# Four strips at a time: scores and products of two units issued together in two attention stages

## The chip, the cores and the metric

The kernel runs on one core of one Trainium2 chip. What is measured is the device time of one execution of the whole program, in microseconds (us), of the slowest core; here that is the only one. A core has a matrix engine (TensorE, PE in the profile, with its weight loads as PEld), a vector engine (VectorE, DVE), a scalar engine (ScalarE, ACT), GpSimd (POOL) and queues for transfers (SyncE, SP). Each engine works through its own list of instructions in order, and they wait for one another by semaphores. TensorE writes to eight banks of PSUM, and the other engines read them from there.

## The reference, cut to what matters

A decoder of four layers with three sublayers each runs on x of 8 sequences x 256 tokens x 256 features, in float32. After each sublayer x becomes the normalised sum of x and the sublayer's result. Two of the twelve sublayers are touched, both in the last layer: a self-attention of 8 heads of 32, behind a normalisation of its own (the kernel calls it grouped), and a cross-attention of 16 heads of 16 over a context of 120 rows, with sigmoids in the place of the softmax.

```python
def _L3_attn_ref(x, Wq, bq, Wk, bk, Wv, bv, gamma, beta):      # H = 8, dk = 32
    ...
    q = (xn @ Wq + bq).reshape(B, S, H, dk).transpose(0, 2, 1, 3)
    k = (xn @ Wk + bk).reshape(B, S, H, dk).transpose(0, 2, 1, 3)
    v = (xn @ Wv + bv).reshape(B, S, H, D).transpose(0, 2, 1, 3)
    scores = jnp.einsum('bhsd,bhtd->bhst', q, k) / jnp.sqrt(jnp.asarray(dk, x.dtype))
    p = jax.nn.softmax(scores, axis=-1)
    att = jnp.einsum('bhst,bhtd->bhsd', p, v)
    out = att.reshape(S, B, D, H).sum(axis=-1).reshape(B, S, D)
    return out

def _L3_xattn_ref(q, k, v, Wq, Wk, Wv, gq, bq, gk, bk, Wp, bp):  # NUM_HEADS = 16, D = 16
    ...
    qh = _layernorm(qh, gq, bq) * scale
    kh = _layernorm(kh, gk, bk)
    attn = jax.nn.sigmoid(jnp.einsum('bhqd,bhkd->bhqk', qh, kh))
    x = jnp.einsum('bhqk,bhkd->bhqd', attn, vh)
    ...
    return x @ Wp.T + bp
```

## The kernel before

The program is one function per sublayer, one after the other. x stays on the chip. In both stages each engine has a loop over steps `t`, and in each step a fixed list of conditions says which piece of which batch or unit it issues; `at_step(t - a, every, count)` gives the piece's number when step `t` is its turn. So the order on every engine is written out by hand, and a piece that waits holds up everything behind it on its engine.

**Grouped attention** (`grouped_attention`, lines 3512 to 3855). A batch is one sequence of 256 tokens. A unit is two heads of one batch: 4 units to a batch, 32 in all, and two units are a quad (16 of them). The work of a unit, by function:

- `scores(u)` (line 3617), TensorE: four matmuls, two heads by two tiles of 128 query rows, each with 32 rows of contraction and 256 columns. The two heads lie on two different strips of 32 rows of the array. A float32 matmul shows as two passes, so a unit's scores are 8 MATMUL records. They go to two banks of PSUM, 0 and 1 for even units, 2 and 3 for odd ones. Unit `u` waits for the exponentials of unit `u - 2`.
- `maxima(u)` (3794), VectorE, then `exps(u)` (3715), ScalarE, from those banks into `probs`.
- `turn_probs(u)` (3629), TensorE: eight transposes into banks 4 and 5. It waits for the exponentials of its own unit and for both copies of the unit before.
- `store_probs(u)`: bank 4 is copied by ScalarE (3724), bank 5 by VectorE (3803). Each is the last piece of its step but for `store_k` on ScalarE.
- `products(u)` (3644), TensorE: four matmuls with 32 output columns each, on two strips of columns, 8 records, into bank 6. It waits for both copies of its unit, and in even units for `out_stored`.
- per quad: `store_out` (3730, ScalarE), `turn_out` (3651, TensorE), `normalise` (3811 and 3816, VectorE).

Once per batch come, through bank 7 and each waiting for the one before to have been copied out: `turn_x` (3578), `project("q")`, `project("k")`, `project_v` (these three through `mm`, line 461) and `turn_tail` (3603) on TensorE, with `store_x`, `store_k` and `store_tail` on ScalarE and `store_q` (3775) and `store_v` (3785) on VectorE. VectorE has besides `pre_statistics` (3751 to 3758), `pre_normalise`, `residual` (3824), `batch_statistics` (831 to 838) and `batch_normalise` (853) once per batch.

**Sigmoid attention** (`sigmoid_attention`, 3858 to 4165). A unit is four heads, 4 units to a batch, 32 in all. `scores(u)` (3962) is four matmuls on two strips of 32 rows, 8 records, again with banks 0 and 1 for even and 2 and 3 for odd units; `sigmoids(u)` (4045, ScalarE) reads them; `products(u)` (3977) is four matmuls, each on a column strip of its own. Per batch: `project_q`, `project_kv`, `output` (line 461), `turn_q` (3940), `turn_k` (3948) and `batch_turn` (862) on TensorE, `store_raw_q` (4015, 4018), `store_raw_k` and `store_q` (4035) on ScalarE, and `variance_q` to `residual` on VectorE.

Of the kernel before, what the change touches and what calls it, by code (L numbers as in the profile page):

```python
# [24 lines left out]
P = 128  # L25
B, L, D = 8, 256, 256
LC = 120
# [6 lines left out]
KT = D // P  # L34
# [839 lines left out]
def at_step(t, every, count):  # L874

    return t // every if t >= 0 and t % every == 0 and t // every < count else None
# [2635 lines left out]
def grouped_attention(nc, K):  # L3512
    W, S, A = weights_of(K, 9), K.S, Arena(K)
    H, HD = 8, 32
    PAIRS, LEAD = 4, 6
    UNITS, QUADS = B * PAIRS, B * PAIRS // 2
    BACK = LEAD + 12
    STEPS = PAIRS * (B - 1) + BACK + 3
    TB, X, Y = (4, 5), 6, 7

    qT, kT, xs = A(2, KT, L), A(2, KT, L), A(2, KT, L)
    vh, xn = A(2, 2, H, HD), A(2, 2, D)
    probs, probsT = A(2, 2, 2 * L), A(2, 2, 2 * L)
# [14 lines left out]
    def heads(u):  # L3538

        return [2 * (u % PAIRS) + s for s in range(2)]  # L3540

    with turn(nc, K) as block:
# [25 lines left out]
        def _(pe):  # L3568
# [35 lines left out]
                                                  K.x_tok[:, 2 * b + i, k * P:(k + 1) * P], K.ident[:])  # L3604
                ins.then_inc(S.aux_done, 1)

            def scores(u):
                b = u // PAIRS
                if u % PAIRS == 0:
                    pe.wait_ge(S.q_stored, b + 1)  # L3610
                    pe.wait_ge(S.k_stored, b + 1)
                if u >= 2:
                    pe.wait_ge(S.probs_done, u - 1)
                for i in range(2):
                    for s, h in enumerate(heads(u)):
                        rows = slice(HD * (h % 4), HD * (h % 4) + HD)
                        ins = nc.tensor.matmul(K.bank[2 * (u % 2) + s][:, i * L:(i + 1) * L],
                                               qT[rows, b % 2, h // 4, i * P:(i + 1) * P], kT[rows, b % 2, h // 4, :],
                                               start=True, stop=True)
                ins.then_inc(S.scores_done, 1)  # L3620

            def turn_probs(u):
                pe.wait_ge(S.probs_done, u + 1)
                for s in range(2):
                    if u:
                        pe.wait_ge((S.pair0_stored, S.pair1_stored)[s], u)
                    for k in range(2):
                        for i in range(2):
                            ins = nc.tensor.transpose(K.bank[TB[s]][:, k * L + i * P:k * L + (i + 1) * P],
                                                      probs[:, u % 2, s, i * L + k * P:i * L + (k + 1) * P], K.ident[:])  # L3630
                    ins.then_inc(S.probsT_done, 1)

            def products(u):
                b, n = u // PAIRS, u // 2
                pe.wait_ge(S.pair0_stored, u + 1)
                pe.wait_ge(S.pair1_stored, u + 1)
                if u % PAIRS == 0:
                    pe.wait_ge(S.v_stored, b + 1)
                if u % 2 == 0 and n:
                    pe.wait_ge(S.out_stored, n)  # L3640
                for k in range(2):
                    for s, h in enumerate(heads(u)):
                        rows = slice(HD * (h % 4), HD * (h % 4) + HD)
                        ins = nc.tensor.matmul(K.bank[X][rows, 0:L], vh[:, b % 2, k, h, :],
                                               probsT[:, u % 2, s, k * L:(k + 1) * L], start=k == 0, stop=k == 1)
                ins.then_inc(S.out_done, 1)

            def turn_out(n):
                pe.wait_ge(S.outT_stored, n + 1)
# [6 lines left out]
            for n, w in enumerate((W["gamma"], W["beta"])):  # L3656
                for k in range(KT):
                    ins = nc.tensor.transpose(K.bank[Y][:, 2 * n + k:2 * n + k + 1], w[0:1, 0, k * P:(k + 1) * P],
                                              K.ident[0:1, 0:1])
            ins.then_inc(S.aux_done, 1)  # L3660
            for t in range(STEPS):
                if (b := at_step(t - BACK - 2, PAIRS, B)) is not None:
                    turn_tail(b)
                if (u := at_step(t - LEAD, 1, UNITS)) is not None:
                    scores(u)
                if (b := at_step(t - 2, PAIRS, B)) is not None:
                    turn_x(b)
                if (b := at_step(t - 3, PAIRS, B)) is not None:
                    project("q", W["wq"], b)
                if (u := at_step(t - LEAD - 1, 1, UNITS)) is not None:  # L3670
                    turn_probs(u)
                if (n := at_step(t - LEAD - 4, 2, QUADS)) is not None:
                    turn_out(n)
                if (b := at_step(t - 4, PAIRS, B)) is not None:
                    project("k", W["wk"], b)
                if (b := at_step(t - 5, PAIRS, B)) is not None:
                    project_v(b)
                if (u := at_step(t - LEAD - 2, 1, UNITS)) is not None:
                    products(u)

        @block.scalar
        def _(a):
# [175 lines left out]
def sigmoid_attention(nc, K):  # L3858
    W, S, A = weights_of(K, 10), K.S, Arena(K)
    H, HD, PAD = 16, 16, 32  # L3860
    QUADS, LEAD = 4, 8
    UNITS = B * QUADS
# [24 lines left out]
    with turn(nc, K) as block:  # L3887
# [23 lines left out]
        def _(pe):  # L3911
# [37 lines left out]
                                              K.ident[0:LC, 0:LC])  # L3949
                ins.then_inc(S.aux_done, 1)  # L3950

            def scores(u):
                b, n = divmod(u, QUADS)
                if n == 0:
                    pe.wait_ge(S.q_stored, b + 1)
                    pe.wait_ge(S.k_stored, b + 1)
                if u >= 2:
                    pe.wait_ge(S.probs_done, u - 1)
                for s in range(2):
                    for r in range(2):  # L3960
                        rows = slice(PAD * (2 * (n % 2) + r), PAD * (2 * (n % 2) + r) + PAD)
                        ins = nc.tensor.matmul(K.bank[2 * (u % 2) + r][0:LC, s * L:(s + 1) * L],
                                               kz[rows, b % 2, s, n // 2, :], qT[rows, b % 2, n // 2, :],
                                               start=True, stop=True)
                ins.then_inc(S.scores_done, 1)

            def products(u):
                b, n = divmod(u, QUADS)
# [22 lines left out]
            for t in range(STEPS):  # L3991
                if (b := at_step(t - 7, QUADS, B)) is not None:
                    turn_k(b)
                if (b := at_step(t - BACK - 3, QUADS, B)) is not None:
                    batch_turn(nc, pe, K, b, Z)
                if (u := at_step(t - LEAD, 1, UNITS)) is not None:
                    scores(u)
                if (b := at_step(t, QUADS, B)) is not None:
                    project_q(b)
                if (b := at_step(t - 1, QUADS, B)) is not None:  # L4000
                    project_kv(b)
                if (b := at_step(t - 6, QUADS, B)) is not None:
                    turn_q(b)
                if (b := at_step(t - BACK, QUADS, B)) is not None:
                    output(b)
                if (u := at_step(t - LEAD - 1, 1, UNITS)) is not None:
                    products(u)
# [1089 lines left out]
```

## Time and profile before

| | us |
|---|---|
| median of 3 runs | 2608.3 (2607.41 to 2608.42) |
| the profiled execution | 2611.01 |
| its span in the trace | 2609.3 |
| PE busy | 2247.2 (86%) |
| DVE busy | 1418.8 (54%) |
| ACT busy | 1056.3 (40%) |
| mean clock granted to TensorE | 0.926 of full speed |

The span runs from the first to the last instruction of the trace. Grouped attention lies at about 1484 to 1672 us of it, sigmoid attention at about 1672 to 1837 us. Busy time is the union of an engine's instructions; an idle engine off the path that sets the time costs nothing. In a timeline a row is a run of like instructions on one engine: start, length from the first start to the last end, engine, line, operation, what it writes and reads, how many records, and in brackets how long the engine had been idle and what ended that. On TensorE a row's length includes the pipeline behind its last pass, so the next row may start before it ends.

### The profile page before, as it was taken

What the parts mean: (1) busy time and instruction counts of PE and PEld (TensorE: products, weight loads), DVE (VectorE), ACT (ScalarE), POOL (GpSimd) and SP (SyncE); (2) the same over time, 40 slices, a digit from 0 to 9 for tenths busy, and PEclk for the clock granted to TensorE, in tenths of its full rate; (3) what the DMA queues carried; (4) which work ended last, traced back from release to release, by engine and by line L of the source; (5) the groups of instructions that cost most, each with busy time, mean ns of one, the idle gap of its engine ahead of it and who ended that gap; (6) DMA issues with size and microseconds to landing.
All of it is one profiled execution on the core that took longest, in us unless ns stands there. A gap on an engine that the chain in (4) does not pass through costs nothing. (4 is left out here: it accounts for less than half of the span.)

```text
span 2609.3 us, 37476 instructions
## 1 busy us (share of the span) xinstructions
PE 2247.2 (86%) x12648; PEld 1631.2 (63%) x12648; DVE 1418.8 (54%) x4103; ACT 1056.3 (40%) x2653; POOL 700.6 (27%) x673
## 2 busy tenths in 40 slices
PE   7995399978869959995699799698899799899898
PEld 5773277755547748883378566365465587465687
DVE  3566022246658947757133566544777443777455
ACT  2443011126525620045034166343567543567532
POOL 1012411110004424411634200363444200534111
PEclk9997699979969979997899899899999899999899
DMA  9114211067000010030254301400000000000000
GB/s 237 39 50 176 91 45 44 23 142 70 1 7 1 1 43 1 19 134 3 93 150 129 129 17 29 168 1 23 11 1 1 1 1 1 1 1 1 21 25 21
DMA packets 112235, 127.29 MB, mean 49 GB/s; under 512 B 46515, under 2 KB 100021, under 8 KB 110256
## 3 DMA queue, kind: packets, MB, share of 16 engines
q1 hardware_dynamic: 103312, 103.91, 14.9%
q0 software_dynamic: 8736, 20.99, 2.2%
q8 instruction: 105, 1.72, 0.3%
q14 instruction: 82, 0.67, 0.1%
HBM read 79.93 MB, written 47.90 MB: 49 GB/s over the span
## 5 line engine op out<-in xcount | busy, mean ns | idle before, releaser
L461 PE MATMUL bank<-weights,work 128*128 128x256 f32 (+5 forms) x1768 | 454.0, 394 | 17.1 <-DVE weights L2542 8.1
L461 PE MATMUL bank<-work,weights 128*128 128x256 f32 (+2 forms) x1552 | 394.4, 406 | 19.7 <-DVE work L4785 12.5
L461 PEld LDWEIGHTS bank<-weights,work 128*128 128x128 f32 (+2 forms) x1768 | 319.8, 192 | 99.6 <-issue 49.4
L461 PEld LDWEIGHTS bank<-work,weights 128*128 128x128 f32 x1552 | 294.7, 195 | 91.9 <-DVE work L4785 16.9
L845 POOL TENSOR_TENSOR work<-work,minus_half 128x2 f32<-128x2 f32 x96 | 69.5, 724 | 837.4 <-DVE work L838 837.4
L461 PE MATMUL bank<-weights,x_feat 128*128 128x512 f32 (+2 forms) x576 | 213.0, 504 | 14.8 <-ACT weights L4389 9.1
L870 ACT COPY x_feat<-bank 128x512 f32<-128x512 f32 x80 | 46.7, 586 | 298.8 <-PE bank L862 298.4
L461 PEld LDWEIGHTS bank<-weights,x_feat 128*128 128x128 f32 x576 | 107.3, 198 | 73.2 <-issue 48.3
L4413 ACT ACTIVATE work<-work 128x128 f32<-128x128 f32 (+1 forms) x256 | 137.6, 547 | 0.2
L461 PE MATMUL bank<-x_feat,weights 128*128 128x256 f32 (+3 forms) x400 | 117.8, 472 | 20.0 <-PEq L247 15.2
L1775 DVE TENSOR_TENSOR work<-bank,work 128x384 f32<-128x384 f32 (+1 forms) x64 | 31.4, 491 | 189.8 <-ACT work L1693 189.8
L461 PE MATMUL bank<-weights 128*128 128x256 f32 (+1 forms) x560 | 129.2, 387 | 1.6 <-ACT weights L4432 0.9
L4485 DVE CUSTOM_DVE_ANT_0 work<-bank,work 128x128 f32<-128x128 f32 (+1 forms) x256 | 76.2, 355 | 77.9 <-PE bank L4304 77.5
L461 PEld LDWEIGHTS bank<-weights 128*128 128x128 f32 x560 | 107.3, 197 | 17.2 <-ACT weights L4432 1.4
L461 PE MATMUL bank<-work 128*128 128x256 f32 (+3 forms) x390 | 88.9, 363 | 29.8 <-ACT work L3004 7.8
L461 PEld LDWEIGHTS bank<-x_feat,weights 128*128 128x128 f32 (+1 forms) x400 | 78.4, 214 | 48.3 <-issue 22.6
L862 PE MATMUL bank<-ident,x_tok 128*128 128x128 f32 x320 | 57.7, 312 | 44.9 <-DVE x_tok L853 42.8
L461 PEld LDWEIGHTS bank<-work 128*128 128x128 f32 (+2 forms) x390 | 65.8, 197 | 44.0 <-issue 13.0
L4255 POOL TENSOR_TENSOR work<-work,minus_half 128x8 f32<-128x8 f32 x32 | 52.4, 1638 | 151.2 <-DVE work L4518 151.2
L1593 POOL DMA_INDIRECT rows_back<-work x40 | 39.0, 974 | 195.2 <-DVE work L1783 191.5
L4795 DVE SCALAR_TENSOR_TENSOR work<-bank,weights,work 128x256 f32<-128x256 f32 x96 | 45.5, 481 | 82.2 <-ACT work L4733 81.6
L1693 ACT ACTIVATE work<-bank 128x384 f32<-128x384 f32 (+1 forms) x64 | 28.1, 438 | 146.2 <-PE bank L461 146.2
(460 smaller groups left out, 4582.2 us busy)
## 6 DMA issues: line engine op xcount, KB each, us to landing
weights<-in_weights SPq DMA_DIRECT2D x1, 12296.0 KB
weights<-in_weights SPq DMA_DIRECT2D x1, 9360.0 KB
weights<-in_weights SPq DMA_DIRECT2D x1, 8488.0 KB
work<-rows_in SPq DMA_DIRECT2D x62, 129.0 KB
rows_in<-ident SPq DMA_DIRECT2D x2, 3968.0 KB, 42.3
weights<-rows_back SPq DMA_DIRECT2D x8, 768.0 KB, 5.2
work<-rows_in SPq DMA_DIRECT2D x8, 645.0 KB, 4.2
rows_in<-ident SPq DMA_DIRECT2D x2, 2560.0 KB, 33.2
```

Of the source, the lines that this page charges most:

```text
L461: ins = nc.tensor.matmul(out, lhsT, rhs, start=(i == 0), stop=(i == len(pairs) - 1))
L845: nc.gpsimd.tensor_tensor(t.rstd[:, n, :], t.rstd[:, n, :], K.minus_half[:, 0:2], ALU.pow).then_inc(K.S.rstd_done, 1)
L862: ins = nc.tensor.transpose(K.bank[bank][:, (2 * k + i) * P:(2 * k + i + 1) * P], K.x_tok[:, 2 * b + i, k * P:(k + 1) * P], K.ident[:])
L870: copy(K.x_feat[:, :, b * L:(b + 1) * L], K.bank[bank][:, :].rearrange("p (k t) -> p k t", k=KT)).then_inc(K.S.xT_stored, 1)
L1593: nc.gpsimd.indirect_dma_start(K.rows_back, bass.IndirectOffsetOnAxis(ap=to, axis=0), y[:, r, :], None, bounds_check=TOP * T - 1, oob_is_e ...
L1693: nc.scalar.activation(gelu[:, at % 2, 0:n], K.bank[2 * (at % 2)][:, 0:n], ACT.Gelu).then_inc(S.gelu_done, 1)
L1775: nc.vector.tensor_tensor(hT[:, q % 2, m, 0:n], K.bank[2 * (at % 2) + 1][:, 0:n], gelu[:, at % 2, 0:n], ALU.mult).then_inc(S.inner_stored, 1)
L4255: nc.gpsimd.tensor_tensor(rk, norm[:, 1, :], K.minus_half[:, 0:H], ALU.pow).then_inc(S.rk_done, 1)
L4413: ins = nc.scalar.activation(probs[:, u % 3, s, at:at + width], probs[:, u % 3, s, at:at + width], ACT.Exp, bias=bias[:, u % 2, i, s:s + 1 ...
L4485: ins = nc.vector.tensor_tensor_reduce(probs[:, u % 3, s, at:at + width], K.bank[SM[s]][:, at:at + width], seen[:, at:at + width], 1.0, -3 ...
L4795: nc.vector.scalar_tensor_tensor(out=hid[rows, b % 2, f, :], in0=K.bank[n % RING][rows, 0:L], scalar=W["b1"][rows, layer, f:f + 1], in1=ge ...
```

## The change

In grouped attention `scores` takes a quad: eight matmuls, the query tile outside and four heads inside, on four strips of rows and into banks 0 to 3. It waits for the exponentials of all units before (`probs_done` at `2 * n`), and raises `scores_done` by 2. `products` takes a quad too: for each of two tiles of keys the four heads on four strips of columns. It waits for the copies of both units. In TensorE's step list `products` moves ahead of `turn_x` and the projections, one step later in time than before for the quad's first unit, and `scores` moves behind `turn_probs`. In sigmoid attention `scores` takes two units in the same way; the other pieces and the step list keep their places. No other engine's code changes. The number of matmuls, their shapes and their results are those of before.

```diff
-            def scores(u):
-                b = u // PAIRS
-                if u % PAIRS == 0:
+            def scores(n):
+                b, m = divmod(n, KT)
+                if m == 0:
                     pe.wait_ge(S.q_stored, b + 1)
                     pe.wait_ge(S.k_stored, b + 1)
-                if u >= 2:
-                    pe.wait_ge(S.probs_done, u - 1)
+                if n:
+                    pe.wait_ge(S.probs_done, 2 * n)
                 for i in range(2):
-                    for s, h in enumerate(heads(u)):
-                        rows = slice(HD * (h % 4), HD * (h % 4) + HD)
-                        ins = nc.tensor.matmul(K.bank[2 * (u % 2) + s][:, i * L:(i + 1) * L],
-                                               qT[rows, b % 2, h // 4, i * P:(i + 1) * P], kT[rows, b % 2, h // 4, :],
-                                               start=True, stop=True)
-                ins.then_inc(S.scores_done, 1)
+                    for j in range(4):
+                        rows = slice(HD * j, HD * j + HD)
+                        ins = nc.tensor.matmul(K.bank[j][:, i * L:(i + 1) * L], qT[rows, b % 2, m, i * P:(i + 1) * P],
+                                               kT[rows, b % 2, m, :], start=True, stop=True)
+                ins.then_inc(S.scores_done, 2)
...
-            def products(u):
-                b, n = u // PAIRS, u // 2
-                pe.wait_ge(S.pair0_stored, u + 1)
-                pe.wait_ge(S.pair1_stored, u + 1)
-                if u % PAIRS == 0:
+            def products(n):
+                b, m = divmod(n, KT)
+                pe.wait_ge(S.pair0_stored, 2 * n + 2)
+                pe.wait_ge(S.pair1_stored, 2 * n + 2)
+                if m == 0:
                     pe.wait_ge(S.v_stored, b + 1)
-                if u % 2 == 0 and n:
+                if n:
                     pe.wait_ge(S.out_stored, n)
                 for k in range(2):
-                    for s, h in enumerate(heads(u)):
-                        rows = slice(HD * (h % 4), HD * (h % 4) + HD)
-                        ins = nc.tensor.matmul(K.bank[X][rows, 0:L], vh[:, b % 2, k, h, :],
-                                               probsT[:, u % 2, s, k * L:(k + 1) * L], start=k == 0, stop=k == 1)
-                ins.then_inc(S.out_done, 1)
+                    for j in range(4):
+                        ins = nc.tensor.matmul(K.bank[X][HD * j:HD * j + HD, 0:L], vh[:, b % 2, k, 4 * m + j, :],
+                                               probsT[:, j // 2, j % 2, k * L:(k + 1) * L], start=k == 0, stop=k == 1)
+                ins.then_inc(S.out_done, 2)
...
                     turn_tail(b)
-                if (u := at_step(t - LEAD, 1, UNITS)) is not None:
-                    scores(u)
+                if (n := at_step(t - LEAD - 3, 2, QUADS)) is not None:
+                    products(n)
...
                     turn_probs(u)
+                if (n := at_step(t - LEAD, 2, QUADS)) is not None:
+                    scores(n)
...
                     project_v(b)
-                if (u := at_step(t - LEAD - 2, 1, UNITS)) is not None:
-                    products(u)
...
-            def scores(u):
-                b, n = divmod(u, QUADS)
-                if n == 0:
+            def scores(pair):
+                b, m = divmod(pair, KT)
+                if m == 0:
                     pe.wait_ge(S.q_stored, b + 1)
                     pe.wait_ge(S.k_stored, b + 1)
-                if u >= 2:
-                    pe.wait_ge(S.probs_done, u - 1)
+                if pair:
+                    pe.wait_ge(S.probs_done, 2 * pair)
                 for s in range(2):
-                    for r in range(2):
-                        rows = slice(PAD * (2 * (n % 2) + r), PAD * (2 * (n % 2) + r) + PAD)
-                        ins = nc.tensor.matmul(K.bank[2 * (u % 2) + r][0:LC, s * L:(s + 1) * L],
-                                               kz[rows, b % 2, s, n // 2, :], qT[rows, b % 2, n // 2, :],
-                                               start=True, stop=True)
-                ins.then_inc(S.scores_done, 1)
+                    for r in range(4):
+                        rows = slice(PAD * r, PAD * r + PAD)
+                        ins = nc.tensor.matmul(K.bank[r][0:LC, s * L:(s + 1) * L], kz[rows, b % 2, s, m, :],
+                                               qT[rows, b % 2, m, :], start=True, stop=True)
+                ins.then_inc(S.scores_done, 2)
...
-                if (u := at_step(t - LEAD, 1, UNITS)) is not None:
-                    scores(u)
+                if (pair := at_step(t - LEAD, 2, UNITS // 2)) is not None:
+                    scores(pair)
```

## Rows read from the trace of the kernel before

**Rows 1.** Windows of grouped and sigmoid attention: length, PE, PEld, DVE, ACT, POOL busy, clock.

```profile
1484.00:1674.00 190.00, 160.99 (x1060) 111.06 (x1060) 124.32 (x279) 101.44 (x345) 13.09 (x19) 0.93 0.15 34
1674.00:1837.00 163.00, 142.24 (x872) 89.74 (x872) 76.39 (x181) 64.29 (x119) 90.54 (x41) 0.93 0.17 69
```

**Rows 2.** Timeline of PE in grouped attention, from a batch in mid-stage.

```profile
1564.23 1.06 PE L3644 MATMUL bank<-work 128*32 128x256 f32 x8
1565.22 0.66 PE L3603 MATMUL bank<-ident,x_tok 128*128 128x128 f32 x4
1565.80 1.13 PE L3617 MATMUL bank<-work 32*128 32x256 f32 x8
1566.87 1.09 PE L3629 MATMUL bank<-ident,work 128*128 128x128 f32 x8
1567.80 0.38 PE L3651 MATMUL bank<-ident,work 128*128 128x128 f32 x2
...
1572.82 1.89 PE L461 MATMUL bank<-work 128*128 128x256 f32 x8
...
1579.10 1.06 PE L3644 MATMUL bank<-work 128*32 128x256 f32 x8 [0.66 <-DVE work L3816]
...
1581.15 1.99 PE L461 MATMUL bank<-work,weights 128*128 128x256 f32 x8
...
1585.52 1.13 PE L3617 MATMUL bank<-work 32*128 32x256 f32 x8
```

**Rows 3.** Timeline of DVE in the same batch of grouped attention.

```profile
1566.98 1.29 DVE L3794 TENSOR_REDUCE work<-bank 128x2 f32<-128x512 f32 x2 [1.74 <-PE bank L3617]
...
1568.76 0.74 DVE L3751 BATCH_NORM_STATS2 work<-x_tok 128x6 f32<-128x256 f32 x2
...
1569.89 0.69 DVE L3803 COPY work<-bank 128x512 f32<-128x512 f32 x1
...
1574.74 0.69 DVE L3785 TENSOR_TENSOR work<-bank,work 128x512 f32<-128x512 f32 x1 [0.81 <-PE bank L461]
1575.65 0.69 DVE L3803 COPY work<-bank 128x512 f32<-128x512 f32 x1 [0.21 <-DVE work L3785]
...
1578.87 0.68 DVE L3824 TENSOR_TENSOR x_tok<-x_tok,work 128x512 f32<-128x512 f32 x1
...
1580.73 0.69 DVE L3803 COPY work<-bank 128x512 f32<-128x512 f32 x1
...
1583.18 0.88 DVE L3775 TENSOR_SCALAR work<-bank,weights 128x256 f32<-128x256 f32 x2
1584.27 0.69 DVE L3803 COPY work<-bank 128x512 f32<-128x512 f32 x1 [0.21 <-DVE work L3775]
```

**Rows 4.** Timeline of ACT there: a unit's first exponential, and the copy behind its last.

```profile
1568.31 0.47 ACT L3715 ACTIVATE work<-bank,work 128x256 f32<-128x256 f32 x1 [1.81 <-DVE work L3794]
...
1570.12 0.60 ACT L3724 COPY work<-bank 128x512 f32<-128x512 f32 x1
```

**Rows 5.** Timeline of PE late in grouped attention: a tail's transposes behind a gap.

```profile
1663.90 1.12 PE L3603 MATMUL bank<-ident,x_tok 128*128 128x128 f32 x4 [4.00 <-DVE x_tok L853]
```

**Rows 6.** Timeline of PE in sigmoid attention, over one batch.

```profile
1750.53 0.64 PE L3977 MATMUL bank<-work 120*32 120x256 f32 x8
1751.10 1.13 PE L3962 MATMUL bank<-work 32*120 32x256 f32 x8
...
1757.41 1.99 PE L461 MATMUL bank<-work,x_feat 128*128 128x256 f32 x8
...
1760.96 1.12 PE L461 MATMUL bank<-work,ctx_feat 128*120 128x256 f32 x4
...
1766.90 1.13 PE L3962 MATMUL bank<-work 32*120 32x256 f32 x8
```

**Rows 7.** Timeline of ACT in the same batch: a unit's sigmoids, and the raw queries' copy.

```profile
1753.80 1.09 ACT L4045 ACTIVATE work<-bank 120x512 f32<-120x512 f32 x2 [0.17 <-ACT work L4035]
...
1759.93 0.58 ACT L4018 COPY work<-bank 128x512 f32<-128x512 f32 x1
```

## The prediction

> **What bounds the kernel now.** I read the busy time in the two stretches that the change touches, and then the timelines of three engines inside them. Grouped attention takes 190 us, of which TensorE is busy 161, VectorE 124 and ScalarE 101; sigmoid attention takes 163 us with 142, 76 and 64 [rows 1]. Both have two ramps, so the middle matters more. There the reader should look at TensorE's timeline [rows 2]: each row starts before the one ahead of it has ended, and in one batch the only idle time is 0.66 us, ahead of a `products`. The scores of a batch's unit start at 1565.80 and those of the same unit one batch later at 1585.52, so a batch takes **19.72 us**, and the sum of TensorE's work sets it. In sigmoid attention a batch takes 1766.90 - 1751.10 = **15.80 us**, packed as densely [rows 6]. So less TensorE time would be worth having, if nothing else is waited for in its place. VectorE is idle for 1.74 us ahead of a maximum, and what ends that idle time is the scores [rows 3]: today VectorE and ScalarE wait for TensorE and have slack.
>
> **What is removed.** Eight passes one behind another on the full array take 1.99 us, the eight passes of a unit's scores on two strips 1.13 us [rows 2], and eight passes on four strips of columns in the sigmoid products 0.64 us [rows 6]. From 1.99 to 1.13 four turns drop out, 0.215 us each; from 1.13 to 0.64 two, 0.245 each. So strips run side by side, two of rows or four of columns. After the change a quad's scores are sixteen passes in four turns. If four strips of rows also run together, they last what a unit's scores last now, 1.13 us, and one scores row in two goes. A scores row costs TensorE 1.07 us from its start to the next row's, a products row 0.99 [rows 2]. Per batch that removes 2 x (1.07 + 0.99) = 4.1 us in grouped attention, and 2 x 1.07 = 2.1 us in sigmoid attention, whose products already use four strips.
>
> No row shows four strips of rows at once. The bounds are four in one turn (the column strips' row) and two at a time, as now: then a quad's scores need four turns more, 4 x 0.215 = 0.86 us. I take four at once, since the column strips do it. The Trainium skill, page TensorE: Matmul & The Clock Gate, section Measured speedup vs the span model, gives 3.07 times for four row tiles and not 4; by that the sixteen passes, some 3.7 us in a row, would take 1.2 us, and the sum would be about 1 us higher. No run here shows it.
>
> **What is added in grouped attention: a wait that closes a loop.** Before, unit `u` wrote its scores while the exponentials of unit `u - 1` ran, because two units had two banks each. Now a quad takes all four banks, so its scores wait for the exponentials of the whole quad before, and TensorE also puts them behind the transposes of its last unit. VectorE must do the maxima of the quad's two units one step apart, with everything of the step between them, and the copy of the *previous* quad's last unit stands behind all that. `products` waits for that copy, and Q or V, the transposes and the next scores are queued behind `products` on TensorE. I follow this round for a batch from the start of the first quad's scores (time 0).
>
> First half, up to the second quad's scores:
> - scores to the start of the maxima: 1566.98 - 1565.80 = 1.18 [rows 2, 3];
> - maxima and `normalise`, up to VectorE's next piece: 1568.76 - 1566.98 = 1.78 [rows 3];
> - residual and statistics: 1580.73 - 1578.87 = 1.86 [rows 3];
> - the copy, 0.69 and 0.05 to hand over (an estimate): 0.74. Time 5.56;
> - `products`: 0.99 [rows 2]. Time 6.55;
> - Q, from its start to that of `store_q`: 1583.18 - 1581.15 = 2.03 [rows 2, 3]. Time 8.58;
> - `store_q` until the bank is given back, between its length 0.88 and VectorE's next start 1.09 behind it [rows 3]; I take 1.0. Time 9.6;
> - the tail's transposes 0.58 (1565.80 - 1565.22), the unit's transposes 1.0 (0.93 to the next row, 1.09 long) [rows 2]. The second quad's scores start at **11.2**.
>
> Second half, up to the next batch's first scores:
> - 1.18 to the maxima, 1568.31 - 1566.98 = 1.33 to the exponentials, 1.81 for these and 0.60 + 0.05 for ScalarE's copy [rows 2 to 4]: 4.97. (VectorE beside it: 1.18 + 1.78, the statistics ahead 1569.89 - 1568.76 = 1.13, copy 0.74: 4.83 [rows 3].)
> - `products` 0.99, transposes 0.93: 6.9;
> - V until `store_v`: 1574.74 - 1572.82 = 1.92; `store_v` until the copy behind it, 0.91; the copy 0.74 [rows 2, 3]: 10.5;
> - half of the transposes waits for that copy: 0.6 (an estimate, half of 1.09 and the gap to the scores). **11.1**.
>
> A batch takes 11.2 + 11.1 = **22.3 us in place of 19.7**. TensorE's sum, 19.72 - 0.66 - 4.1 = 15.0 us, no longer matters. From the first batch's scores to the last's there are seven such intervals, 7 x 2.55 = 18 us. The first batches lack the residual and the tail, but then they also lack it today, so I keep the difference. The last batch loses about 2 us on its first quad and wins back as much, since its last unit comes with the one before: nothing, by 3 us either way. Grouped attention: **+18 us**.
>
> **The clock.** In the first half TensorE has nothing to do from the end of `turn_out` (1.07 + 0.38 = 1.45) until `products` at 5.56: 4.1 us idle in each batch, where now there is 0.66. Behind a gap of 4.00 us four transposes took 1.12 us [rows 5] and not 0.66 [rows 2], so they ran at the lower of the clock's two levels, 1.2 in place of 2.4 GHz. What follows the new gap on the chain is `products`, Q and a unit's transposes, 0.99 + 1.83 + 0.93 = 3.75 us, and the lower level would add at most that much again per batch. Bounds: 0 and 8 x 3.75 = 30 us. The gap is as long as the one of the row, which speaks for some; the level comes back while TensorE is kept busy, so not all of the 3.75 us is slow. I take 1 us per batch, **+8 us**. The Trainium skill, same page, section HAM oscillation, has the rule that waits between bursts of matmuls send the clock back each time; by that rule it would be every batch, which is the second rival.
>
> **Sigmoid attention.** The same wait is added, but no maxima stand on the way. From the second pair's scores (0): its first unit's sigmoids end at 1753.80 + 1.09 - 1751.10 = 3.79 [rows 6, 7], now with no scores to fill the time on TensorE; `products` at 3.9, 0.57 long (1751.10 - 1750.53) [rows 6], the batch's transposes 0.58: the next scores at 5.1, to 6.15. Then Q's projection; the raw copy behind it ends 1759.93 + 0.58 - 1757.41 = 3.10 after its start [rows 6, 7], and the next projection waits for it: 9.3 (today a scores row covers this wait). From there to the next such scores 1766.90 - 1760.96 = 5.94: **15.3 us in place of 15.8** [rows 6]. Of the 2.1 us removed, 0.5 stay: 8 x 0.5 = **-4 us**. Bounds: -17 if all is kept, 0 if another handover is late.
>
> **Sum.** Against the profiled execution's 2611.0 us: +18 + 8 - 4 = +22, 2633; the median of the runs is 2.7 us below that execution, and so I forecast 2608.3 + 22 = **2630 us**. The steps alone leave 2615 to 2640.
>
> **Rivals.**
> 1. *TensorE stays the bound* (faster). Place: `products` behind the new gap. If the copy were there in time, the batch would be 15.0 us, 8 x (15.0 - 19.7) = -38 us, and sigmoid attention -17: **2553 us**. It decides once the round falls under 19.7 us, and is paid in full at 15.0. For it: VectorE and ScalarE are busy 124 and 101 of 190 us. Against: the waits are in order, and the round of 22.3 holds no step that another engine could take. A chance of 0.07.
> 2. *The clock falls behind every gap*: +18 + 30 - 4, up to **2652 us**. For it: the length of the gap. 0.15.
> 3. *Four strips of rows run two at a time*: 0.86 us on the round for each of 16 quads and 16 pairs, 2630 + 28 = **2658 us**. This is also the case that the change doesn't do what it says. For it: only two are seen. 0.06.
> 4. *Part of the round hides*: if V, `store_v` and the copy behind it are ready in time, 2.3 us per batch go, the round is 20.0 and grouped attention about +2, the clock +2, sigmoid -4: **2608 us**. 0.07.
>
> My forecast has 0.65. The range reaches from the lower side of the forecast to the second rival, 2612 to 2652, and leaves out the first, third and fourth. Slower by over 0.2% (5.2 us, about what a measurement of this kernel can tell from none): the forecast, the second and the third, less a little for the forecast's low end, 0.85; within 0.2% 0.07; faster 0.08.
>
> **What would show it.** Right: in grouped attention scores rows of sixteen records, 1.1 to 1.2 us long, 11.1 to 11.2 us apart; TensorE idle for some 4 us ahead of every second `products`, ended by VectorE's copy (3803); VectorE no longer idle for the scores alone; TensorE's busy time in that stretch down by 30 us while the stretch grows to about 215 us; some `products` and Q rows at twice their length if the clock falls. Sigmoid batches of 15.3 us, with a new idle time ahead of the second projection and of `products`. Wrong: a batch of 15 us with TensorE dense (the first rival); scores rows of 2 us (the third); or a round of which VectorE's in-order work is not a part, which would take the floor from the whole argument.

## The result, and the profile after

The changed kernel takes **2643.8 us** (median of 4 runs, 2642.1 to 2646.8) against 2607.9 us before: a ratio of 1.0137, 95% interval 1.0125 to 1.0150, or 36 us more. The forecast was 2630 us in a range of 2612 to 2652.

The page of the changed kernel, and then the two stages from one mark of GpSimd to the next, to within 0.3 us (columns as in [rows 1]: length, busy time of PE, PEld, DVE, ACT and POOL, granted clock, share of the DMA engines and GB/s; line numbers behind the change are lower by two or three):

```profile
span 2645.1 us, 37460 instructions
...
PE 2222.8 (84%) x12648; PEld 1617.7 (61%) x12648; DVE 1417.6 (54%) x4103; ACT 1054.7 (40%) x2653; POOL 699.6 (26%) x673
```

```profile
1487.20:1709.00 221.80, 148.46 (x1063) 106.08 (x1061) 121.87 (x277) 101.70 (x345) 11.13 (x17) 0.85 0.11 26
1709.00:1855.10 146.10, 115.16 (x848) 75.22 (x848) 70.79 (x164) 59.08 (x113) 84.45 (x34) 0.93 0.16 67
```

The same marks in the kernel before:

```profile
1482.40:1669.10 186.70, 161.09 (x1064) 111.11 (x1064) 122.48 (x276) 101.44 (x345) 11.12 (x18) 0.94 0.14 31
1669.10:1818.90 149.80, 130.91 (x848) 85.09 (x848) 71.08 (x163) 60.73 (x113) 85.55 (x36) 0.93 0.16 65
```

TensorE is busy 24 us less over the whole kernel, and the kernel is 36 us slower. Grouped attention goes from 186.7 to 221.8 us (+35.1), although TensorE's busy time there falls by 12.6, and the granted clock falls from 0.94 to 0.85. Sigmoid attention goes from 149.8 to 146.1 (-3.7). The remaining 4.5 us of the profiled execution lie ahead of both stages (the first mark stands at 1482.4 and at 1486.9), in code that is the same in both kernels; more on that below. By the marks, sigmoid attention ended at 1818.9 us before the change and not at 1837: the second window of [rows 1] reaches 18 us into the next sublayer, so its 163 us are 149.8. No term of the forecast used that length.

One batch of grouped attention after the change, TensorE's timeline (start, length, engine, line, operation, tiles, count, idle time ahead and what ended it). It answers to [rows 2]:

```profile
1600.68 1.15 PE L3617 MATMUL bank<-work 32*128 32x256 f32 x16
1601.76 0.44 PE L3649 MATMUL bank<-ident,work 128*128 128x128 f32 x2
...
1606.33 1.27 PE L3642 MATMUL bank<-work 128*32 128x256 f32 x16 [4.13 <-DVE work L3801]
1607.54 3.43 PE L461 MATMUL bank<-work,weights 128*128 128x256 f32 x8
1610.80 1.04 PE L3628 MATMUL bank<-ident,work 128*128 128x128 f32 x8
1612.09 0.63 PE L3603 MATMUL bank<-ident,x_tok 128*128 128x128 f32 x4 [0.25 <-DVEq L3777]
1612.55 1.04 PE L3628 MATMUL bank<-ident,work 128*128 128x128 f32 x8
1613.52 1.15 PE L3617 MATMUL bank<-work 32*128 32x256 f32 x16
...
1618.52 1.07 PE L3642 MATMUL bank<-work 128*32 128x256 f32 x16 [1.75 <-ACT work L3722]
1619.52 1.09 PE L3628 MATMUL bank<-ident,work 128*128 128x128 f32 x8
1620.45 1.89 PE L461 MATMUL bank<-work 128*128 128x256 f32 x8
1623.27 0.63 PE L3578 MATMUL bank<-ident,work 128*128 128x128 f32 x4 [0.93 <-DVEq L3787]
1623.73 1.04 PE L3628 MATMUL bank<-ident,work 128*128 128x128 f32 x8
1624.70 1.15 PE L3617 MATMUL bank<-work 32*128 32x256 f32 x16
```

A quad's sixteen score passes take 1.15 us, what a unit's eight took. But the rows no longer touch: 4.13 us of idle time end with VectorE's copy (3801), 1.75 with ScalarE's (3722), 0.93 when `store_v` has given its bank back. From scores to scores it is 12.83 us and then 11.18, a batch of 24.0 us where it was 19.7. Q's row at 1607.54 takes 3.43 us where [rows 2] has 1.99. VectorE in the same batch, beside [rows 3]:

```profile
1601.90 1.29 DVE L3792 TENSOR_REDUCE work<-bank 128x2 f32<-128x512 f32 x2 [1.94 <-PE bank L3617]
...
1603.67 0.68 DVE L3822 TENSOR_TENSOR x_tok<-x_tok,work 128x512 f32<-128x512 f32 x1
1604.39 0.75 DVE L831 BATCH_NORM_STATS2 work<-x_tok 128x6 f32<-128x256 f32 x2
...
1605.54 0.69 DVE L3801 COPY work<-bank 128x512 f32<-128x512 f32 x1
1606.14 1.28 DVE L3792 TENSOR_REDUCE work<-bank 128x2 f32<-128x512 f32 x2
```

The copy that `products` waits for starts at 1605.54, behind the maxima, the residual and the statistics, though the transposes it reads were done by 1600.8. The clock, by windows of the same trace: the stretch of the idle time, and the one behind it.

```profile
1603.90:1607.40 3.50, 1.07 (x16) 0.50 (x16) 3.40 (x10) 1.73 (x7) 0.69 (x1) 0.95 0.00 0
1607.40:1610.80 3.40, 3.40 (x12) 2.63 (x9) 0.67 (x3) 1.93 (x8) 0.00 (x0) 0.55 0.00 0
```

TensorE idled through most of the first of these, with the clock granted in full but for the edge (0.95), and worked through the second at the lower level: a granted 0.55 is 1.2 GHz but for the edges.

Sigmoid attention after, TensorE over one batch and then ScalarE's sigmoids of the second pair, beside [rows 6, 7]:

```profile
1789.23 1.14 PE L3960 MATMUL bank<-work 32*120 32x256 f32 x16
...
1793.08 0.64 PE L3974 MATMUL bank<-work 120*32 120x256 f32 x8 [0.73 <-ACT work L4042]
...
1794.24 1.14 PE L3960 MATMUL bank<-work 32*120 32x256 f32 x16
...
1798.47 1.12 PE L461 MATMUL bank<-work,ctx_feat 128*120 128x256 f32 x4 [0.59 <-ACT work L4015]
...
1804.41 0.92 PE L3960 MATMUL bank<-work 32*120 32x256 f32 x12
```

```profile
1791.94 2.06 ACT L4042 ACTIVATE work<-bank 120x512 f32<-120x512 f32 x4 [0.17 <-ACT work L4032]
```

From 1789.23 to 1804.41 a batch takes 15.18 us, and the two new waits stand where the prediction put them: 0.73 us ahead of a `products`, 0.59 ahead of the second projection.

### The profile page after: what moved, and what is told of

Same layout as the page of the kernel before. It is cut to its first block and busy times, and to the rows that moved or that the text cites. A ratio compares the mean times of both kernels' runs of the same rounds, so it can differ in the third digit from the quotient of the medians.

```text
span 2645.1 us, 37460 instructions
## 1 busy us (share of the span) xinstructions
PE 2222.8 (84%) x12648; PEld 1617.7 (61%) x12648; DVE 1417.6 (54%) x4103; ACT 1054.7 (40%) x2653; POOL 699.6 (26%) x673
## 5 line engine op out<-in xcount | busy, mean ns | idle before, releaser
L461 PE MATMUL bank<-work,weights 128*128 128x256 f32 (+2 forms) x1552 | 404.3, 413 | 19.5 <-DVE work L4782 12.3
L461 PEld LDWEIGHTS bank<-work,weights 128*128 128x128 f32 x1552 | 301.4, 199 | 96.7 <-DVE work L4782 16.7
L461 PE MATMUL bank<-x_feat,weights 128*128 128x256 f32 (+3 forms) x400 | 117.6, 471 | 20.1 <-PEq L247 15.4
L1775 DVE TENSOR_TENSOR work<-bank,work 128x384 f32<-128x384 f32 (+1 forms) x64 | 31.4, 491 | 190.2 <-ACT work L1693 190.2
L461 PEld LDWEIGHTS bank<-weights 128*128 128x128 f32 x560 | 107.8, 198 | 17.5 <-ACT weights L4429 1.4
```

The source lines that it names most:

```text
L461: ins = nc.tensor.matmul(out, lhsT, rhs, start=(i == 0), stop=(i == len(pairs) - 1))
L1775: nc.vector.tensor_tensor(hT[:, q % 2, m, 0:n], K.bank[2 * (at % 2) + 1][:, 0:n], gelu[:, at % 2, 0:n], ALU.mult).then_inc(S.inner_stored, 1)
```

## The experiments

**The two stages apart.** First the grouped stage as changed beside the sigmoid stage of before, then the other way round.

> The grouped stage as changed, the sigmoid stage as before. If grouped attention carries the whole loss and sigmoid attention gives 4 us back, this is 4 us above the changed kernel: 2648 us, its batches 24.0 us apart and sigmoid batches 15.8. If sigmoid attention had lost too (its stage disturbed by the same wait), it would be below 2640 us.

> The sigmoid stage as changed, the grouped stage as before. If the two stages add up: 2604 us, 4 below the kernel before, with sigmoid batches of 15.2 us. If all of the TensorE time removed there were kept (2.1 us per batch) it would be 2591 us; if the gain in this stage comes only from what the grouped stage leaves behind, it is 2608 us.

Measured: grouped alone 2643.3 us (ratio 1.0133, 1.0118 to 1.0149), its stages 219.4 and 149.1 us. Sigmoid alone 2606.0 us against 2608.3 (0.9988, 0.9979 to 0.9997), its stages 187.2 and 146.2 us. So grouped attention carries the whole loss, and the sigmoid stage gains by its marks 3.6 us beside the old grouped stage and 3.0 beside the new one. In whole runs that gain is small beside the spread: 2 us by the medians here, and 2643.3 against the changed kernel's 2643.8 shows none.

The changed grouped code took 221.8 us in the changed kernel's trace and 219.4 here: 1.8 of these 2.4 us lie in the opening, from the stage's first mark to its first scores, another 1.8 in the first batch, and the rest comes back later. The granted clock goes with it, first the changed kernel's opening and then this run's:

```profile
1486.90:1508.60 21.70, 13.47 (x46) 9.23 (x46) 12.78 (x23) 3.03 (x6) 1.50 (x4) 0.61 0.19 67
```

```profile
1482.20:1502.00 19.80, 11.28 (x44) 8.07 (x44) 12.78 (x23) 3.03 (x6) 1.45 (x4) 0.74 0.20 73
```

So a difference of some 2 us between two grouped stages, each profiled once, need not come from their code.

**Which part of grouped attention.** First the new scores with the products of before, in their old place at the end of the step:

```diff
-                if (n := at_step(t - LEAD - 3, 2, QUADS)) is not None:
-                    products(n)
...
+                if (u := at_step(t - LEAD - 2, 1, UNITS)) is not None:
+                    products(u)
```

> Grouped attention with the scores by quad behind the transposes, as changed, but the products by unit and last in the step, as before; sigmoid stage as before. If the loss comes from products by quad standing ahead of Q and V and waiting there for the late copy (2 us per batch on the round and the gap that lowers the clock), a batch takes 20.3 us and the kernel 2612 us, with no gap near 4 us on TensorE. If the scores' wait for all four banks is the cause by itself, a batch stays at 22 to 24 us and the kernel at 2630 to 2645 us.

```profile
1485.10:1677.10 192.00, 144.63 (x1060) 99.37 (x1060) 121.44 (x277) 101.02 (x345) 11.12 (x17) 0.95 0.13 30
```

Measured: 2619.0 us (1.0040, 1.0025 to 1.0055), the stage 192.0 us, scores 10.26 and 10.32 us apart, a batch of 20.6, and the stage's clock at 0.95. The wait of the scores for all four banks, with their place behind the transposes, costs 0.9 us per batch and 5 us in the stage. It is not the main cause by itself. The medians are 10.7 us apart, twice what the stage shows; the profiled execution was the fastest one of its kernel.

Then the other half: products by quad, behind Q and ahead of the transposes, with the scores by unit of before.

```diff
+                if (n := at_step(t - LEAD - 3, 2, QUADS)) is not None:
+                    products(n)
                 if (u := at_step(t - LEAD - 1, 1, UNITS)) is not None:
                     turn_probs(u)
...
-                if (u := at_step(t - LEAD - 2, 1, UNITS)) is not None:
-                    products(u)
```

> Grouped attention with the products by quad on four strips of columns, behind Q and ahead of the transposes, but the scores by unit as before, with their two pairs of banks; sigmoid stage as before. If TensorE is the bound as long as the scores run ahead, a batch loses 2 x 0.99 us and the idle 0.66: 17.1 us, the kernel 2588 us. If products by quad are harmful wherever they stand (their copy is always late), a batch is 20 us or more and the kernel 2612 us or more.

```profile
1484.00:1661.50 177.50, 151.68 (x1061) 108.75 (x1060) 121.89 (x277) 100.58 (x345) 11.11 (x17) 0.89 0.14 33
```

Measured: 2599.7 us (0.9963, 0.9949 to 0.9976), the stage 177.5 us and a batch 18.2 us (four gaps between scores of 6.59, 4.03, 4.82 and 2.74). So the quad's products are a gain of 9 us by the marks (8 from the first scores on) when they don't stand in front of the work that could fill their wait. I had expected 17.1 us per batch; the tail's transposes still waited for `store_q` (0.63 us), and the last batch fell to the lower clock.

**What is queued behind the wait.** The changed kernel with that one call moved, and nothing else:

```diff
-                if (n := at_step(t - LEAD - 3, 2, QUADS)) is not None:
-                    products(n)
                 if (b := at_step(t - 2, PAIRS, B)) is not None:
                     turn_x(b)
                 if (b := at_step(t - 3, PAIRS, B)) is not None:
                     project("q", W["wq"], b)
+                if (n := at_step(t - LEAD - 3, 2, QUADS)) is not None:
+                    products(n)
```

> The changed kernel with one call moved: in grouped attention the products of a quad stand behind turn_x and project q, just ahead of the transposes. If the loss hangs on what is queued behind the waiting products, Q fills the gap (no fall of the clock there) and drops out of the round: halves of 10.3 and 11.1 us, a batch of 21.4 and not 24.0, the grouped stage some 201 us and the kernel 2622 us. If the place of the products does not matter and the four banks do, the stage stays at 215 us or more and the kernel at 2640 us.

```profile
1615.53 1.89 PE L461 MATMUL bank<-work,weights 128*128 128x256 f32 x8
1619.83 1.07 PE L3642 MATMUL bank<-work 128*32 128x256 f32 x16 [2.40 <-DVE work L3801]
```

Measured: 2621.6 us (1.0050, 1.0033 to 1.0068); halves of mostly 10.32 and 11.18 us, the stage 204.6. The row at 1615.53 is Q, now inside the gap; what is left of it, 2.40 us, no longer brings the clock down each time (`products` at 1619.83 takes 1.07). One line's place was worth 17 us of the stage's 35.

**The clock.** Eight matmuls without a reader go into the gap. They write the bank of the projections, behind a wait that its last content has been copied:

```diff
             def products(n):
                 b, m = divmod(n, KT)
+                if n % 2:
+                    pe.wait_ge(S.aux_stored, before_step[2 * n + LEAD + 3])
+                    for _ in range(8):
+                        nc.tensor.matmul(K.bank[Y][:, 0:L], K.ident[:], W["wq"][:, 0, :], start=True, stop=True)
```

> The changed kernel, with eight matmuls of 128x256 whose result nobody reads put into TensorE's gap ahead of every second products in grouped attention, about 3.5 us of the 4.1; the output is unchanged. If the fall of the clock behind that gap costs 1.65 us per batch, the longer halves shrink from 12.83 to 11.2 us and the kernel takes 2631 us. If the slower products and Q rows are hidden anyway, or the fill delays the products, it stays at 2644 us or above.

```profile
1611.55 1.15 PE L3618 MATMUL bank<-work 32*128 32x256 f32 x16
1612.63 0.44 PE L3654 MATMUL bank<-ident,work 128*128 128x128 f32 x2
1612.90 3.62 PE L3638 MATMUL bank<-weights,ident 128*128 128x256 f32 x16
1617.20 1.07 PE L3647 MATMUL bank<-work 128*32 128x256 f32 x16 [0.68 <-ACT work L3727]
1618.20 1.99 PE L461 MATMUL bank<-work,weights 128*128 128x256 f32 x8
```

```profile
1484.80:1692.10 207.30, 158.50 (x1192) 118.02 (x1190) 121.86 (x277) 101.44 (x345) 11.11 (x17) 0.95 0.12 28
```

Measured: 2629.9 us, the stage 207.3 us, both halves 11.18 to 11.19 us, the clock 0.95. More work on TensorE makes the stage 14.5 us shorter than in the changed kernel's trace, and 12.1 shorter than in the run with the grouped stage alone (219.4), whose opening is as long as here. The waits are untouched (`products` comes 5.65 us after the scores, as in the changed kernel); only `products` and Q are back to 1.07 and 1.99 us. So the changed kernel's 221.8 us are 186.7 + 20.6 for the round + 14.5 for the clock, and of these 14.5 us 10.7 lie in the first halves of the last seven batches, behind the gap. The other 3.7 lie in the opening and in the first batch (1.8 each), ahead of the first such gap; the run with the grouped stage alone lost nothing there, and 11.6 us in the seven first halves.

**The late copy.** The copies of odd units are moved ahead of the maxima and the exponentials, on both engines; the even ones stay:

```diff
+                if (u := at_step(t - LEAD - 1, 1, UNITS)) is not None and u % 2:
+                    store_probs(u)
                 if (u := at_step(t - LEAD, 1, UNITS)) is not None:
                     maxima(u)
...
-                if (u := at_step(t - LEAD - 1, 1, UNITS)) is not None:
+                if (u := at_step(t - LEAD - 1, 1, UNITS)) is not None and u % 2 == 0:
                     store_probs(u)
```

> The changed kernel, with the copies of every odd unit's probabilities (VectorE's and ScalarE's) moved ahead of the maxima and exponentials of the step, where both engines wait for the scores anyway. If the late copy behind VectorE's in-order work is what the round hangs on, the halves fall to 9.7 and 9.6 us, the gap ahead of products goes, the clock stays up, and the kernel takes 2600 us. If the four banks alone make the round, it stays above 2625 us.

```profile
1601.33 0.69 DVE L3803 COPY work<-bank 128x512 f32<-128x512 f32 x1 [0.84 <-PE bank L3628]
1602.44 1.29 DVE L3794 TENSOR_REDUCE work<-bank 128x2 f32<-128x512 f32 x2 [0.41 <-PE bank L3617]
...
1603.87 0.42 DVE L3816 TENSOR_TENSOR work<-bank,work 128x256 f32<-128x256 f32 x1
```

```profile
1604.44 1.07 PE L3642 MATMUL bank<-work 128*32 128x256 f32 x16 [1.70 <-DVE work L3816]
```

Measured: 2610.2 us, the same as before (0.9995, 0.9980 to 1.0009); the stage 193.0 us, the halves 9.70 and 9.71. The copy runs while VectorE waits for the scores anyway, the idle time ahead of `products` is 1.70 us and ended by `normalise`, which must free bank 6. Without any change to TensorE's code, 29 us of the 35 are gone. The batches are where I expected them, the kernel is 10 us above my figure: a batch of 19.4 us saves only 0.3 against before, and the first and the last batches, with nothing else to fill the waits, still run at the lower clock for parts (stage clock 0.87).

**Two strips at a time.** I tried to price the four strips by issuing heads 0 and 1 for both tiles, and then heads 2 and 3:

```diff
-                for i in range(2):
-                    for j in range(4):
+                for i, j in ((0, 0), (0, 1), (1, 0), (1, 1), (0, 2), (0, 3), (1, 2), (1, 3)):
```

> The changed kernel, with the eight score matmuls of a quad in grouped attention issued two strips at a time (heads 0 and 1, then 2 and 3). If the scores lie on the round, each of the sixteen quads costs 0.86 us more, 14 us in all: 2658 us. If they are not on it, 2644 us. It also measures what four strips at once are worth: scores rows of 2.0 us and not 1.15.

```profile
1608.94 1.16 PE L3616 MATMUL bank<-work 32*128 32x256 f32 x16
```

Measured: 2639.6 us, the stage 222.3 us, and the sixteen passes take 1.16 us. Neither 2658 us nor rows of 2.0 us came, but that says nothing on whether the scores lie on the round, as the experiment did not do what it was for: in the trace four records still start within 0.033 us of the first of a group, and the next four follow 0.32 us behind it. Heads 2 and 3 must have overtaken what was queued ahead of them on the other strips, since two strips at a time would need eight turns and the length allows four. What two strips at a time would cost in this loop was therefore not measured.

**Towards a better version.** The two parts that gain, together; then `turn_tail` behind the scores of its step; then five matmuls without a reader ahead of the products of the quads 13 and 15.

> Products by quad in grouped attention with the scores by unit, and sigmoid attention as changed: the sum of the two parts that should gain. If they add up, 2584 us, about 4 below the run with the products alone.

> The best kernel so far (products by quad behind Q, scores by unit in grouped attention, sigmoid attention as changed) with turn_tail behind the scores of its step and not ahead: the idle 0.63 us of TensorE there, until store_q has given the bank back, lies beside the scores. 0.6 us in each of five batches: 3 us less, 2589 us. If VectorE and the in-order waits set this loop's time by now, it stays at 2592 us.

> The same, with five matmuls of 128x256 whose result nobody reads ahead of the products of the quads 13 and 15, where TensorE waits 2.3 to 3.1 us at the end of the stage and the clock then stays at the lower level for 17 us. If that is what slows the end, 4 to 6 us less than without them: 2584 us. If the end is set by VectorE and the transfers, no difference.

```profile
1484.20:1654.50 170.30, 144.62 (x1062) 104.17 (x1060) 121.35 (x278) 101.02 (x345) 11.13 (x17) 0.92 0.15 34
```

Measured: 2592.1 us (0.9927, 0.9904 to 0.9949), 2589.8 us (0.9934, 0.9909 to 0.9959) and 2588.7 us (0.9924, 0.9905 to 0.9942), each against the kernel before on its own chip. By the stage's marks, grouped attention takes 176.8, 170.3 and 169.4 us. The tail's place gave the 3 us expected in the steady batches (0.7 in each of four, as a batch went from 18.2 to 17.5 us). The other 3.9 us are in the last batch, which went from 38.5 to 34.6 us as the granted clock rose from 0.66 to 0.78; that the tail's place did that is not shown.

The filled end looks like 0.9 us, but its opening, in code that is the same, was 2.2 us longer (20.1 against 17.9, at a clock of 0.58 against 0.71). From the last batch's first scores to the stage's end, first without and then with the fill:

```profile
1619.40:1654.00 34.60, 17.97 (x141) 12.05 (x140) 20.93 (x53) 13.34 (x45) 2.68 (x4) 0.78 0.15 31
```

```profile
1623.10:1654.60 31.50, 20.34 (x161) 14.10 (x160) 20.93 (x53) 13.21 (x45) 2.68 (x4) 0.92 0.17 34
```

There the fill gave 3.1 us at a higher clock. So the rival, that VectorE and the transfers set the end, does not hold for the whole of it, though less came than the 4 to 6 us expected. The whole runs don't tell the three apart. All three beat both kernels, by 19 to 20 us against before and 52 to 55 us against the change.

## Why the prediction was right, step by step

**The removed TensorE time.** Right. Four strips of rows run at once: 1.15 us for sixteen passes, against my 1.13. By the Trainium skill's 3.07 times for four row tiles (page TensorE: Matmul & The Clock Gate, section Measured speedup vs the span model) the estimate was 1.2 us; the trace has a little less. By the third rival's own count of sixteen quads and sixteen pairs that estimate would have added some 2 us to the sum and not 1. Sixteen passes on four strips of columns take 1.07. The third rival is out.

**The round.** Right in both lengths, and by its own edges in the first half. I had 11.2 and 11.1 us for the halves; with the clock kept up they measure 11.19 and 11.18. `products` was to start 5.56 us after the scores, it starts 5.65 after them (1606.33 - 1600.68).

In the second half the agreement is in part luck. `products`, V and `store_v` came as added up, but my last edge, half of the transposes waiting for VectorE's copy, is not the one that binds in a mid-stage batch. I had left `turn_x` out: it waits until `store_v` has given bank 7 back (the 0.93 us at 1623.27), and its 0.46 us and a full row of transposes, 0.97, come behind it, by which time the copy is done. The two ways happen to differ by 0.1 us. Only the last second half has no `turn_x`; there my edge does bind, and it takes 11.10 us (1672.64 - 1661.54):

```profile
1670.20 0.60 PE L3628 MATMUL bank<-ident,work 128*128 128x128 f32 x4
1672.06 0.66 PE L3628 MATMUL bank<-ident,work 128*128 128x128 f32 x4 [1.25 <-DVE work L3801]
```

The fourth rival is out, since nothing of V and `store_v` was hidden; the first is as well, since the stage's TensorE time fell without any gain. It fell by 12.6 us and not by the 30 that I named, as the lower clock lengthens what is left: with the clock kept up, and the extra matmuls not counted, it is 131 us against 161, the 30 less.

In the stage the round comes to 20.6 us, where I had 18. The seven intervals come to 19.0: the first batch, which I gave the same difference as the others, loses 3.5 us, not 2.55 (19.1 from scores to scores with the clock kept up, 15.6 before). The last batch and the end, which I put at nothing, cost 1.4, and the opening 0.2.

**The clock.** This is the term that was mis-sized, +8 for a measured 14.5 us, of which 10.7 (11.6 in the run with the grouped stage alone) lie behind the gaps. I had the place and the cause, but took 1 us per batch where a fall costs more and comes each time: the seven first halves that have the gap are longer than in the run with the filled gap by 0.3 to 2.4 us, three of the four with a residual and a tail by 1.64 us. The price for one fall was well inside my bounds, since only about 1.65 us of the 3.75 on the chain were added before the clock was back. The Trainium skill's rule (page TensorE: Matmul & The Clock Gate, section HAM oscillation), that such waits between bursts of matmuls send the clock back each time, was the better guide to how often; the trace agrees, with a fall behind each of the seven gaps. The second rival had that mechanism, and with its upper price its 2652 us is nearer to the measured 2643.8 than my 2630 (8 us against 14). The steps of the forecast alone left 2615 to 2640 us; the range holds the result because it was drawn up to that rival.

**Sigmoid attention.** Right: 15.2 us per batch against my 15.3, -3.7 us against -4, and both new waits where I had put them.

**The sum.** 20.6 + 14.5 - 3.7 = 31.4 us from the two stages, where I had 22. The medians differ by 36 us. The other 4.5 us lie ahead of both stages, in code that is the same: grouped attention begins at 1482.4, 1484.6, 1486.9 and 1489.0 us in the profiled executions of before, of the filled gap, of the change and of the moved products. The steps go with the clock. The marks cut the code ahead into six stretches. From before to the change, the third, fifth and sixth grow by 2.3, 1.7 and 2.5 us, TensorE's busy time in them by 2.3, 2.2 and 1.7, and each has a granted clock lower by 0.01; the first is 2.1 us shorter. What makes the clock come out differently in like code stays open. The medians of the change and of the grouped stage alone both stand 35 to 36 us above before, so a part of this may belong to these kernels after all; one profile of each cannot tell.

**What the experiments add to the argument.** I had followed one round and said what it costs; I had not said which of its edges to cut. The same late copy could be made harmless from either end: by letting Q go ahead of the waiting `products` (17 us of the stage), or by copying earlier (29 us). And the order in which two edits were made together hid that one of them, the products by quad, was good by itself.

## What to carry to other kernels

Work that is removed from the busiest engine counts only if what it waits for next is earlier than the end of that work. Two units issued together on one set of banks give up the banks' double use: follow one whole round, from the wait back to itself, through every piece that stands in order ahead of the releasing one on the other engines, before trusting the busy shares. Put what doesn't depend on a late result ahead of the instruction that waits for it, and a copy that frees others ahead of work that nobody waits for; and count a gap like the one of 4.13 us here twice, once as time and once as the slower matmuls behind it (1.64 us in a steady batch).

## What the runs showed of the hardware that I had not expected

- Extra matmuls with no reader, 3.6 us per batch in a gap of 4.1 us, made a stage 12 to 14.5 us shorter (219.4 in one trace of that code and 221.8 in another, to 207.3), by keeping TensorE's clock at its higher level.
- Matmuls on different strips of rows don't start in the order in which they were issued. With four matmuls on strips 0 and 1 ahead of those on strips 2 and 3, the first passes of all four strips start within 0.033 us, the second passes 0.32 us later, and sixteen passes take 1.16 us, as in the other order (1.15). The records don't name their strips; that they are the four strips' is read from the count and the length.
- The same code ahead of the changed stages ends up to 7 us apart in different profiled executions, with the granted clock lower where it takes longer. Marks help as far as the clock in a stage repeats: sigmoid attention took 149.1 to 149.8 us in four traces of its old code and 145.3 to 146.8 in nine of the new, but one and the same grouped code took 219.4 and 221.8, and an opening of the same code 17.9 and 20.1.
